# Output weight loaded behind the second exchange, and the last FP4 weight pieces loaded by GpSimd's queue

## The chip, the cores and the metric

One core of a Trainium2 chip runs the whole kernel in one launch. The metric is the device time in microseconds (us); lower is better. Before the change three runs gave a median of 1065.6 us (1063.15 to 1066.27).

## The reference

x has 4 batches of 1024 tokens with 256 features, all in float32. Cut to what matters (rmsnorm multiplies by a weight):

```
xn = layernorm(x)
# branch 1: linear attention (8 heads of 128, chunks of 128), then a SwiGLU MLP (1024)
h = rmsnorm(xn, attn_norm_w);  q, k, v = h@Wq, h@Wk, h@Wv      # per head
for each chunk:  o = tril(q k^T) v + q S;   S = S + k^T v
y = xn + rmsnorm(o, attn_out_norm_w) @ Wo
h = rmsnorm(y, mlp_norm_w)
s = y + (silu(h@Wgate) * (h@Wup)) @ Wdown
# branch 2: FP4 network; fq rounds groups of 16 to the FP4 grid, scaled by the group's maximum
a = silu(fq(xn) @ fq(w_gate)^T) * (fq(xn) @ fq(w_up)^T)        # 704 wide
out = x + s * silu(fq(a) @ fq(w_down)^T)
```

## The kernel before

Every float32 product is made of three products of rounded parts (high and low), each weight and activation being split once: ScalarE writes the high part, VectorE subtracts it for the low part. All products go through `split_product`, whose line is L263.

**Stages.** The first half of the run is attention; the second half, from about 605 us, is the MLP and the FP4 network together (`networks`). Attention goes through 4 batches, each with 16 head steps: step j is head j % 8 of the half batch (512 tokens, a "block") j // 8. In step j TensorE makes the scores of step j (L720), the keys, queries and values of step j+1 and later (L263), the state products (L750), the output from the masked scores (L765) and from the states (L771), and the output projection of step j-2 (L263). ScalarE copies results out of PSUM, squares outputs for the norm (L962) and rounds high parts. VectorE masks scores (L1518), sums states (L1542), normalizes outputs (L1563, L1558), and between these does the statistics of the next block (L1248 and on) and the FP4 rounding.

**The exchange.** The state products need the keys with tokens on the partitions. Instead of transposing on TensorE, each step sends keys and normalized outputs through DRAM: SP writes them in one transfer of 512 KB (L406, `moved<-work`), waits for it, and reads them back in four of 128 KB (L414, `r_gate<-moved`); VectorE then transposes blocks of 32x32 (L1389 for keys, L1506 for outputs). `exchange(value)` waits for the reads of the exchange before, for ScalarE's permuted keys (`k_perm_ready`) and for the normalized output (`o_norm_ready`).

**What sets the order.** Every engine's program is written out by hand and is executed in order; engines meet at semaphores only. All transfers but three small ones at the start are issued by SP, so they stand in one queue. SP's part of a step is `attention_transfers(b, j, first, final)`: the exchange first, then in some steps gate and up weights (h == 0), the store of x2 (`kept`), of the quantized x (`kept_xq`), of the normed h2 (`kept_h2`), and the loads and stores of FP4 weight pieces. Ahead of the loop stand the loads of x and of the q, k and v weights, exchange 1, the output weight `Wo` (1 MB, L496) and x of block 1 (L498).

**The output weight.** `raw_out` is its landing place. ScalarE rounds half of it in each of head steps 0 and 1 of the first batch (`weight_out_hi`, L1032) and VectorE takes the rest in steps 1 and 2 (`weight_out_lo`, L1320). TensorE needs the first half in step 2 and the second in step 6.

**FP4 weight pieces.** The three FP4 weights are cut in six pieces, which are rounded to the grid and turned during attention. Pieces 0 and 1 stay on chip. Pieces 2 to 5 are stored in DRAM (`kept_w4`) and are read back in the last batch: pieces 2 and 3 (352 KB each, `raw_gate4`) in step 12 at L454, after the exchange and the two stores of that step; pieces 4 and 5 (384 KB each, `raw_down4`) in step 14 at L468 and L470. ScalarE rounds the first two in step 14 and the others in step 15 (L1022), VectorE follows (L1492).

**GpSimd** (`block.gpsimd`) clears buffers at the start, waits for the q, k and v weights, clears two more, and has then no work until it multiplies and adds the finished rows of the networks.

Of the kernel before, what the change touches and what calls it, by code (L numbers as in the profile page):

```python
# [13 lines left out]
P = 128  # L14
# [44 lines left out]
def build(nc, x, attn_w, Wq, Wk, Wv, Wo, out_w, mlp_w, Wgate, Wup, Wdown, w_gate, w_up, w_down, out):  # L59
    batches, tokens, D = x.shape  # L60
    HD = Wq.shape[1]
    H = HD // P
    KD = D // P
# [7 lines left out]
    CH = BANK // P  # L71
    TB = CH * P
    HALVES = tokens // TB
    BLOCKS = batches * HALVES
# [22 lines left out]
    with ctx:  # L97
# [285 lines left out]
        with nc.Block() as block:  # L383
            @block.sync
            def _(sp):
# [31 lines left out]
                def attention_transfers(b, j, first, final):  # L417
# [3 lines left out]
                    if not (final and j >= STEPS - LAG):  # L421
                        exchange(t0 + j + 2, t0 + j if not first or j else None,
                                 t0 + j - 1 if not first or j >= LAG else None)
                    if h == 0:
                        sp.wait_ge(gu_ready, n + 1)
                        if n:
                            sp.wait_ge(xq_stored, 16 * n)
                        else:
                            sp.wait_ge(h_turned, KD)
                        for i, w in enumerate((Wgate, Wup)):  # L430
                            sp.dma_start(gu_piece[:, i, :], w[s * P:(s + 1) * P, b * PIECE:(b + 1) * PIECE])\
                              .then_inc(gu_loaded, 16)
# [17 lines left out]
                    if final and j == STEPS - CH:  # L450
                        sp.wait_ge(piece_stored, 16 * (PIECES - 2))
                        sp.wait_ge(o_done, b * STEPS + STEPS - CH)
                        for k in range(KD):
                            sp.dma_start(raw_gate4[:, k, :], kept_w4[2 + k]).then_inc(w4_loaded, 16)  # L454
# [10 lines left out]
                    if final and j == STEPS - LAG:  # L465
                        sp.wait_ge(piece_stored, 16 * (PIECES - 2))
                        sp.wait_ge(xq_ready, BLOCKS)
                        sp.dma_start(raw_down4[0], kept_w4[4]).then_inc(down4_loaded, 16)  # L468
                        sp.wait_ge(h2_turned, BLOCKS)
                        sp.dma_start(raw_down4[1], kept_w4[5]).then_inc(down4_loaded, 16)  # L470
# [25 lines left out]
                sp.dma_start(raw_out, Wo.rearrange("(h p) n -> p h n", p=P)).then_inc(w_loaded[W_OUT], 16)  # L496
# [77 lines left out]
            def _(pool):  # L574
# [12 lines left out]
                pool.memset(x2, 0.0).then_inc(x2_summed, 1)  # L587

# [322 lines left out]
            def _(act):  # L911
# [157 lines left out]
                def attention(b, j, first, final):  # L1069
# [25 lines left out]
                    if first and j < 2:  # L1095
                        weight_out_hi(j)
# [678 lines left out]
```

## Time and profile before

| what | us |
|---|---|
| median of three runs | 1065.6 |
| the profiled execution | 1068.49 |
| its span, first to last instruction | 1066.8 |
| busy in it: TensorE | 1053.6 |
| busy: VectorE | 905.1 |
| busy: ScalarE | 525.6 |
| busy: GpSimd | 47.2 |

The mean granted TensorE clock was 0.995 of full speed. Times inside a profile are counted from the start of its span; the busy time of TensorE includes time at the lower clock. "SPq" are instructions of SP that issue transfers.

### The profile page before, as it was taken

To read this page: it belongs to the slowest core of one execution; us is meant where nothing else is said; L and a number is where in the kernel's file an instruction comes from. 1 tells how busy PE (TensorE), PEld (TensorE's weight loads), DVE (VectorE), ACT (ScalarE), POOL (GpSimd) and SP (SyncE) were. 2 spreads that over 40 slices of the span, in tenths; PEclk is the share of its full clock that TensorE was granted. 3 is DMA by queue.
4 is the path that set the end of the run, shared out by engine and by line. 5 is a ranking of instruction groups with operands and counts; after the bars stand their busy time and mean duration, and the time that the engine had idled before them with its cause. 6 is when DMAs were issued, how large, how long until landed. Compare 5 with 4: busy or idle time off the path is not lost.

```text
span 1066.8 us, 18798 instructions
## 1 busy us (share of the span) xinstructions
PE 1053.6 (99%) x6790; PEld 965.0 (90%) x6790; DVE 905.1 (85%) x1860; ACT 525.6 (49%) x1482; POOL 47.2 (4%) x68
## 2 busy tenths in 40 slices
PE   9899999999999999999999999999999999999998
PEld 6799999989998999999998889999999999999997
DVE  6788898888887888888887798889888888889887
ACT  6664655755646646557555534443333333243332
POOL 1000000000000000000000000101001010101010
PEclk9999999999999999999999899999999999999999
DMA  7455355455464563654446523243433233423213
GB/s 250 129 153 175 118 170 170 128 162 168 134 189 131 166 185 107 186 167 153 160 129 204 150 65 100 80 149 93 125 93 115 88 120 92 125 86 91 87 57 112
DMA packets 166220, 143.08 MB, mean 134 GB/s; under 512 B 28784, under 2 KB 162928, under 8 KB 166128
## 3 DMA queue, kind: packets, MB, share of 16 engines
q1 hardware_dynamic: 165440, 141.88, 43.4%
q8 instruction: 54, 0.88, 0.4%
q14 instruction: 38, 0.31, 0.1%
q10 hardware_dynamic: 688, 0.00, 0.0%
HBM read 77.27 MB, written 64.57 MB: 133 GB/s over the span
## 4 chain that ended last, share of the span: by engine, by line
PE 94%; DMA 2%; DVE 1%; ACT 1%; issue 1%; SPq 0%; POOL 0%; DVEq 0%; ACTq 0%; POOLq 0%
PE ps L263 72%; PE ps L720 5%; PE ps L765 5%; PE ps L771 5%; PE ps L750 4%; DMA moved<-work 1%; DMA r_gate<-moved 1%; PE ps L854 1%; PE ps L648 1%; PE ps L608 1%; SPq L414 0%; DVE work L1362 0%; DVE work L1389 0%; ACT work L962 0%; DVE work L1506 0%
## 5 line engine op out<-in xcount | busy, mean ns | idle before, releaser
L263 PE MATMUL ps<-r_k,r_gate_up 128*128 128x512 f32 x768 | 185.2, 391 | 0.7 <-DVE r_k L1571 0.7
L263 PEld LDWEIGHTS ps<-r_k,r_gate_up 128*128 128x128 f32 x768 | 141.5, 188 | 28.1 <-issue 0.9
L263 PE MATMUL ps<-r_o,onT 128*128 128x256 f32 x768 | 107.5, 289 | 0.0
L263 PE MATMUL ps<-r_h,r_k 128*128 128x512 f32 (+1 forms) x393 | 105.1, 403 | 0.0
L263 PEld LDWEIGHTS ps<-r_q,r_v 128*128 128x128 f32 x768 | 99.7, 191 | 4.9 <-DVE r_v L1639 0.3
L263 PE MATMUL ps<-r_q,r_v 128*128 128x256 f32 x768 | 102.3, 283 | 0.0
L263 PE MATMUL ps<-r_h,r_q 128*128 128x512 f32 x384 | 98.2, 391 | 0.0
L263 PE MATMUL ps<-r_v,r_h 128*128 128x512 f32 x384 | 97.5, 390 | 0.0
L263 PEld LDWEIGHTS ps<-r_o,onT 128*128 128x128 f32 x768 | 96.5, 191 | 0.1
L962 ACT ACTIVATE work<-ps 128x128 f32<-128x128 f32 x256 | 67.1, 278 | 59.4 <-PE ps L771 59.3
L942 ACT ACTIVATE work<-ps 128x512 f32<-128x512 f32 x63 | 37.7, 598 | 111.3 <-PE ps L263 110.9
L1147 ACT ACTIVATE r_v<-work 128x512 fp32r<-128x512 f32 x64 | 40.5, 633 | 99.1 <-DVE work L1635 99.0
L263 PEld LDWEIGHTS ps<-r_h,r_q 128*128 128x128 f32 x384 | 72.1, 188 | 16.4
L263 PEld LDWEIGHTS ps<-r_v,r_h 128*128 128x128 f32 x384 | 72.1, 188 | 15.0
L1542 DVE TENSOR_TENSOR work<-ps,work 128x128 f32<-128x128 f32 x192 | 55.7, 290 | 32.0 <-ACT work L976 21.8
L263 PEld LDWEIGHTS ps<-r_h,r_k 128*128 128x128 f32 x393 | 68.3, 189 | 11.1
L1143 ACT ACTIVATE work<-ps 128x512 f32<-128x512 f32 x64 | 38.3, 598 | 79.7 <-PE ps L263 79.7
L263 PE MATMUL ps<-r_up,r_k 128*128 128x352 f32 x384 | 71.7, 322 | 0.2 <-DVE work L1558 0.2
L263 PE MATMUL ps<-r_gate,r_k 128*128 128x352 f32 x384 | 71.8, 322 | 0.0
L750 PEld LDWEIGHTS ps<-work 128*128 128x128 f32 x448 | 60.8, 195 | 12.1 <-DVE work L1389 3.9
L765 PE MATMUL ps<-work 128*128 128x128 f32 x512 | 69.3, 280 | 0.0
L750 PE MATMUL ps<-work 128*128 128x128 f32 x448 | 62.0, 280 | 5.8 <-DVE work L1389 3.1
(160 smaller groups left out, 2002.9 us busy)
## 6 DMA issues: line engine op xcount, KB each, us to landing
moved<-work SPq DMA_DIRECT2D x63, 512.0 KB, 2.9
r_gate<-moved SPq DMA_DIRECT2D x252, 128.0 KB, 2.6
kept_h<-work SPq DMA_DIRECT2D x31, 384.0 KB, 2.6
work<-kept_h SPq DMA_DIRECT2D x124, 96.0 KB, 2.3
work<-in_L_attn_hidden_states SPq DMA_DIRECT2D x15, 512.0 KB, 5.4
kept<-work SPq DMA_DIRECT2D x9, 514.0 KB, 4.9
kept_h<-work SPq DMA_DIRECT2D x9, 512.0 KB, 3.7
kept_xq<-work SPq DMA_DIRECT2D x8, 512.0 KB, 5.8
```

The source lines that it names most:

```text
L263: done = pe.matmul(out_ap, a, b, start=first and n == 0, stop=last and n == 2, skip_group_check=skip)
L608: done = pe.transpose(ps[:, H_BANKS[k], c * P:(c + 1) * P], h_sb[:, c, k * P:(k + 1) * P], ident[:, :])
L648: pe.matmul(ps[:, B_O, :], leaving[:, 0, 1, :], leaving[:, :, 1, :], start=True, stop=True)
L720: done = pe.matmul(ps[:, B_SCORE, c * P:(c + 1) * P], kT[:, c * P:(c + 1) * P], qT[:, j % 2, c * P:(c + 1) * P], start=True, stop=True)
L750: done = pe.matmul(ps[:, B_STATE, c * P:(c + 1) * P], k_tok[:, c, :], v_sb[:, half, c, hv:hv + P], start=True, stop=True)
L765: pe.matmul(ps[:, B_O, c * P:(c + 1) * P], attn[:, c, :], v_sb[:, half, c, hv:hv + P], start=c == 0, stop=s == 0 and c == 0, skip_group_ch ...
L771: done = pe.matmul(ps[:, B_O, c * P:(c + 1) * P], qT[:, j % 2, c * P:(c + 1) * P], before, start=False, stop=True, skip_group_check=True)
L942: act.activation(k_perm, ps[:, B_K, :].rearrange("p (c b t) -> p c b t", b=QUADS, t=QUAD), ACT.Copy)\
L962: done = act.activation(squares[:, c, :], ps[:, B_O, c * P:(c + 1) * P], ACT.Square, accum_out=small[:, OS, c:c + 1])
L1143: act.activation(s_gate, ps[:, B_GATE, :], ACT.Silu).then_inc(s_gate_ready, 1)
L1147: act.activation(hmT[:, f % 2, HI, :], hm, ACT.Copy).then_inc(hm_hi, 1)
L1542: dve.tensor_tensor(to, share, last, ALU.add).then_inc(state_ready, 1)
```

## The change

The load of `Wo` moves from behind exchange 1 to step 0 of the first batch, behind exchange 2 and ahead of that step's gate and up weights. ScalarE's two `weight_out_hi` move from steps 0 and 1 to steps 1 and 2. The four loads of `raw_gate4` and `raw_down4` leave SP's program; GpSimd issues them on its own queue, after the same waits, behind its second pair of clears.

```diff
--- before.py
+++ after.py
@@ -421,6 +421,8 @@
                     if not (final and j >= STEPS - LAG):
                         exchange(t0 + j + 2, t0 + j if not first or j else None,
                                  t0 + j - 1 if not first or j >= LAG else None)
+                    if (b, j) == (0, 0):
+                        sp.dma_start(raw_out, Wo.rearrange("(h p) n -> p h n", p=P)).then_inc(w_loaded[W_OUT], 16)
                     if h == 0:
                         sp.wait_ge(gu_ready, n + 1)
                         if n:
@@ -447,11 +449,6 @@
                         sp.wait_ge(xq_stored, 16)
                         sp.wait_ge(x2_summed, BLOCKS)
                         load_turned(xq_in, kept_xq[0], xq_loaded)
-                    if final and j == STEPS - CH:
-                        sp.wait_ge(piece_stored, 16 * (PIECES - 2))
-                        sp.wait_ge(o_done, b * STEPS + STEPS - CH)
-                        for k in range(KD):
-                            sp.dma_start(raw_gate4[:, k, :], kept_w4[2 + k]).then_inc(w4_loaded, 16)
                     if h == CH + 1:
                         sp.wait_ge(h2_turned, n + 1)
                         sp.dma_start(kept_h2[(n + BLOCKS - 1) % BLOCKS].rearrange("a p x -> p a x"), in_quads(h_flat))\
@@ -462,12 +459,6 @@
                         else:
                             sp.wait_ge(w_ready, W_OUT + 2)
                         load_piece(n, range(QUADS // 2) if h == CH + 1 else range(QUADS // 2, QUADS))
-                    if final and j == STEPS - LAG:
-                        sp.wait_ge(piece_stored, 16 * (PIECES - 2))
-                        sp.wait_ge(xq_ready, BLOCKS)
-                        sp.dma_start(raw_down4[0], kept_w4[4]).then_inc(down4_loaded, 16)
-                        sp.wait_ge(h2_turned, BLOCKS)
-                        sp.dma_start(raw_down4[1], kept_w4[5]).then_inc(down4_loaded, 16)
 
                 def load_piece(m, quads):
 
@@ -493,7 +484,6 @@
                         sp.dma_start(in_quads(to)[q * QUAD:(q + 1) * QUAD],
                                      quads[q].rearrange("(b p) x -> p b x", b=QUADS)).then_inc(done_sem, 16)
                 exchange(1, again=False)
-                sp.dma_start(raw_out, Wo.rearrange("(h p) n -> p h n", p=P)).then_inc(w_loaded[W_OUT], 16)
                 sp.wait_ge(xn_ready, 1)
                 sp.dma_start(x_in, x_blocks[1]).then_inc(x_loaded, 16)
                 for j in range(ROLL):
@@ -585,6 +575,16 @@
                 pool.wait_ge(w_ready, W_OUT)
                 pool.memset(attn, 0.0).then_inc(attn_cleared, 1)
                 pool.memset(x2, 0.0).then_inc(x2_summed, 1)
+
+                last = (batches - 1) * STEPS
+                pool.wait_ge(piece_stored, 16 * (PIECES - 2))
+                pool.wait_ge(o_done, last + STEPS - CH)
+                for k in range(KD):
+                    pool.dma_start(raw_gate4[:, k, :], kept_w4[2 + k]).then_inc(w4_loaded, 16)
+                pool.wait_ge(xq_ready, BLOCKS)
+                pool.dma_start(raw_down4[0], kept_w4[4]).then_inc(down4_loaded, 16)
+                pool.wait_ge(h2_turned, BLOCKS)
+                pool.dma_start(raw_down4[1], kept_w4[5]).then_inc(down4_loaded, 16)
 
                 pool.sem_inc(product_ready, 1)
                 for n in range(BLOCKS - 1):
@@ -1092,8 +1092,8 @@
                         copy_v(t0 + j + CH + 1, *((1, h) if h < CH else (0, h - CH)))
                     if s == 0:
                         first_state(t0 + j + 1, b * UPDATES + updates_before(j))
-                    if first and j < 2:
-                        weight_out_hi(j)
+                    if first and j in (1, 2):
+                        weight_out_hi(j - 1)
                     if h == 1:
                         wgate_up_hi(b, s)
                     if h == 2:
```

## Rows read from the trace of the kernel before

**Rows 1.** The page, busy share (part 1) and chain (part 4).

```profile
PE 1053.6 (99%) x6790; PEld 965.0 (90%) x6790; DVE 905.1 (85%) x1860; ACT 525.6 (49%) x1482; POOL 47.2 (4%) x68
...
PE 94%; DMA 2%; DVE 1%; ACT 1%; issue 1%; SPq 0%; POOL 0%; DVEq 0%; ACTq 0%; POOLq 0%
```

**Rows 2.** Timeline of TensorE: start us, us, engine line op out<-in xcount [idle before <-releaser].

```profile
29.94 1.52 PE L263 MATMUL ps<-r_v,r_h 128*128 128x512 f32 x6
34.56 1.88 PE L750 MATMUL ps<-work 128*128 128x128 f32 x8 [3.10 <-DVE work L1389]
36.23 1.92 PE L765 MATMUL ps<-work 128*128 128x128 f32 x8
...
43.74 1.05 PE L750 MATMUL ps<-work 128*128 128x128 f32 x8
44.63 1.06 PE L765 MATMUL ps<-work 128*128 128x128 f32 x8
...
53.12 1.05 PE L750 MATMUL ps<-work 128*128 128x128 f32 x8
...
328.77 1.21 PE L771 MATMUL ps<-work 128*128 128x128 f32 x6 [0.34 <-ACT work L976]
```

**Rows 3.** Slices of half a us: busy (x) of each engine, granted clock, DMA share, GB/s.

```profile
34.50:35.00 0.50, 0.44 (x3) 0.44 (x4) 0.00 (x1) 0.00 (x0) 0.00 (x0) 0.80 0.68 238
```

**Rows 4.** Timeline of SP's queue, first exchanges.

```profile
19.08 0.43 SPq L496 DMA_DIRECT2D work<-in_L_attn_Wo  x1
...
22.00 0.37 SPq L406 DMA_DIRECT2D moved<-work  x1
28.82 1.75 SPq L414 DMA_DIRECT2D r_gate<-moved  x4
```

**Rows 5.** The page, part 6: issue, KB each, median us to landing.

```profile
moved<-work SPq DMA_DIRECT2D x63, 512.0 KB, 2.9
```

**Rows 6.** Timeline of VectorE, first head steps.

```profile
27.48 1.41 DVE L1248 BATCH_NORM_STATS2 work<-work 128x6 f32<-128x256 f32 x4 [1.26 <-DMA work<-in_L_attn_hidden_states]
...
32.52 0.16 DVE L1272 TENSOR_TENSOR work<-work 128x4 f32<-128x4 f32 x1
33.79 0.71 DVE L1389 STREAM_TRANSPOSE work<-r_gate 128x512 f32<-128x512 f32 x1 [1.11 <-DMA r_gate<-moved]
...
52.15 0.71 DVE L1389 STREAM_TRANSPOSE work<-r_gate 128x512 f32<-128x512 f32 x1
```

**Rows 7.** Timeline of ScalarE, head steps 1 and 2.

```profile
36.65 1.14 ACT L1032 ACTIVATE r_o<-work,nw_out 128x1024 fp32r<-128x1024 f32 x1
...
47.39 0.26 ACT L962 ACTIVATE work<-ps 128x128 f32<-128x128 f32 x1
```

**Rows 8.** Timeline of SP's queue, head step 12 of the last batch.

```profile
575.24 2.25 SPq L454 DMA_DIRECT2D work<-kept_w  x2
577.60 0.56 SPq L406 DMA_DIRECT2D moved<-work  x1
583.74 1.74 SPq L414 DMA_DIRECT2D r_gate<-moved  x4
```

**Rows 9.** Timelines of TensorE and of VectorE at the second stop.

```profile
588.41 1.62 PE L750 MATMUL ps<-work 128*128 128x128 f32 x6 [2.72 <-issue]
...
587.60 0.71 DVE L1389 STREAM_TRANSPOSE work<-r_gate 128x512 f32<-128x512 f32 x1 [2.50 <-DMA r_gate<-moved]
```

**Rows 10.** Slices of half a us at attention's end.

```profile
576.50:577.00 0.50, 0.50 (x4) 0.41 (x3) 0.50 (x2) 0.24 (x1) 0.00 (x0) 1.00 0.97 366
...
587.50:588.00 0.50, 0.00 (x0) 0.00 (x0) 0.40 (x1) 0.00 (x0) 0.00 (x0) 0.76 1.06 328
...
594.50:595.00 0.50, 0.50 (x6) 0.50 (x5) 0.01 (x1) 0.47 (x4) 0.00 (x0) 0.92 0.00 0
```

**Rows 11.** Timeline of ScalarE, rounding of the last pieces.

```profile
589.95 1.46 ACT L1022 ACTIVATE r_gate<-work 128x704 fp32r<-128x704 f32 x2
...
597.32 1.58 ACT L1022 ACTIVATE r_h<-work 128x768 fp32r<-128x768 f32 x2
```

## The prediction

> **What bounds the kernel now.** I read the page's busy shares and its chain first: TensorE is busy 99% of the span, and the chain that ended last is 94% TensorE [rows 1]. Time can come only from places where TensorE stands still or runs slowly. Its timeline up to 600 us has two stops longer than 0.4 us behind the start-up: 3.10 us ahead of the state products at 34.56 [rows 2] and 2.72 us at 588.41 [rows 9]. Each edit works on one of them.
>
> Both stops cost more than their length. After the first the granted clock is 0.80 in the slice 34.5 to 35.0 [rows 3] and 0.50 in those that follow: 1.2 instead of 2.4 GHz. The same eight products take 1.88 us at 34.56 and 1.05 at 43.74, the next eight 1.92 and 1.06 [rows 2]: 0.83 + 0.86 = 1.7 us lost, of which about 0.1 hides a wait on the states. At the second stop the clock falls in the slice 587.5 to 588.0 and is back in the slice 594.5 to 595.0 [rows 10]. By the slice means that is about 587.76 to 594.54; the work from 588.41 on is 6.1 us at half rate, so 3.1 us are lost.
>
> I call the exchange that brings head step j its exchange j+1. The loop's step j issues exchange j+2.
>
> **Why the first stop exists.** SP issues the output weight (1 MB) at 19.08, x behind it, and exchange 2's write at 22.00 [rows 4]. That write's issue waits for ScalarE's permuted key, not for the weight. Its reads start at 28.82 [rows 4], so it took 6.8 us; the median of 63 such writes is 2.9 [rows 5]. VectorE transposes at 33.79 [rows 6], TensorE goes on at 34.56.
>
> **Part 1, the weight behind exchange 2.** Without 1 MB ahead, the write takes 2.9 us, or up to 3.8 with the tail of x ahead, and the reads are issued from 25.0 to 25.8. From first read issue to transpose the row has 33.79 - 28.82 = 5.0 us, so the tile is there between 30.0 and 30.8 [rows 4, 6]. Then VectorE is late. Its statistics of the next block began at 27.48 after 1.26 us of waiting for x [rows 6], which also stood behind the weight. With x there they begin at 26.2. From their start to the end of the last small operation ahead of the transpose are 32.52 + 0.16 - 27.48 = 5.2 us, in which nothing waits [rows 6]. So the transpose starts at 31.4, and TensorE, which followed it by 34.56 - 33.79 = 0.77, at 32.1 to 32.2. Gain 2.4 us. TensorE's values end at 29.94 + 1.52 = 31.46 [rows 2], so a stop of 0.7 us is left. A stop of 0.34 us at 328.77 [rows 2] left the clock at 1.0, one of 3.1 did not; I take it that 0.7 does, and the 1.6 us come back as well. Bounds of the clock term: 0 and 1.7.
>
> The rounding of the weight (ScalarE, 1.14 us a half [rows 7]; VectorE 1.2) moves from head steps 0 and 1 to 1 and 2. In step 0 this frees ScalarE, which nobody waits for there. In step 1 the first half takes the place of the second: no change in length, VectorE's part follows right behind. In step 2 there is 1.05 us (1.14 less the overlap of neighbours) of new work ahead of the squares of x2 and of the root of the output norm, which began at 47.39 [rows 7]. VectorE had been late for that root by about 0.1, as it normalized the next block until 49.0, so 0.9 us pass on to its chain and its transpose of step 3. That transpose ran 52.15 to 52.86 [rows 6], 0.26 ahead of TensorE's need at 53.12 [rows 2]; the first state copy and state sums of that step, which the state products need at once, shift by the full 0.9. I take a loss of 0.9 us for TensorE; bounds 0 (if the slack takes it) and 1.2.
>
> The weight is now ahead of exchange 3, with 256 KB of gate and up weights. It is issued at 26.8 to 27.6; 1.25 MB at the 366 GB/s of [rows 10] take 3.6 us and end at 31.4 to 32.3. Exchange 3's write is issued at 29.8 (behind the norm of step 0), lands at 33.3 to 34.1, and its reads (5.0 us) are there by 38.3 to 39.1. VectorE gets to that transpose at 38.5 in the moved time line, TensorE needs its end at 39.8. So the cover is 0.1 to 0.7 us: I take a cost of 0. If it is gone, it costs one for one, up to 2.0 if the weight runs at the pace it had at 19.08, where it shared the engines.
>
> Sum of part 1: -2.4 - 1.6 + 0.9 = -3.1 us.
>
> **Part 2, the FP4 pieces on GpSimd's queue.** In head step 12 of the last batch SP issues two loads of 352 KB at 575.24, then the write of exchange 15 at 577.60, whose reads start only at 583.74 [rows 8]: 6.1 us instead of 2.9. VectorE's transpose follows at 587.60 and TensorE at 588.41 [rows 9]. VectorE itself would be ready at about 585.0, so this stop ends with the transfer throughout. The change takes 0.72 MB out from ahead of that write: they start some 10 us sooner, when step 11's output is done (about 564.9). It puts the first 384 KB of the down weight there instead: GpSimd issues it when the quantized x is turned, about 573.7. The second 384 KB go at about 581.4, between the write's data and its reads. At 366 GB/s [rows 10] that is 2.0 us out and 1.1 in: the write lands 0.9 us sooner, and the stop is 1.8 us. I take -0.9. The bounds: nothing gained or 1 us lost where GpSimd's loads run beside the reads of exchanges 13 and 14, whose transposes have under 0.4 us of cover; and -2.0 if the down piece slips in beside. For the clock I take no change: it fell 2.1 us after the products had stopped, and 1.8 is near.
>
> What comes late now is no risk: ScalarE rounds the pieces at 589.95 and 597.32 [rows 11], 25 and 16 us behind their issue. GpSimd has nothing else to do until the gated products of the networks, so its three new waits block nobody.
>
> The trace of before has no load on GpSimd's queue. The Trainium skill (DMA: Bandwidth & Descriptors, Queues, rings and completion order) says that each DMA engine takes turns between its queues packet by packet. By that rule the bulk loads, which on SP's queue stood in line, take half the engines from an exchange issued beside them; those are cases 3 and 5 below. The skill also says (SBUF - State Buffer, SBUF: two separate sides) that GpSimd cannot write descriptors while VectorE runs certain fast copies. With 16 us of cover and more that changes no number here.
>
> **The sum.** -3.1 - 0.9 = -4.0 us against the profiled execution: 1068.5 (span 1066.8, and 1.7 around it) gives 1064.5. The median of the runs shown is 2.9 us under that execution, so I put it at 1065.6 - 4.0 = 1061.6 us. What a measurement of this kernel can tell from no change is about 0.3%, or 3.2 us.
>
> **The cases.** Four rivals stand around the forecast.
> 1. Both stops shrink and the second leaves the clock up: 3.1 us more. 1061.6 - 3.1 = 1058.5. For it: the stop falls under the 2.1 us after which the clock fell. Against: it is only 0.3 us under, and a stop of 0.7 us would be a safer sign than one of 1.8. 0.20.
> 2. The forecast as above, 1061.6; with its own bounds 1060 to 1063.2. 0.37.
> 3. GpSimd's loads give nothing: they take from exchanges 13 and 14 what they free for 15, and cost 0.4 on top. 1065.6 - 3.1 + 0.4 = 1062.9. For it: these transposes have almost no cover. 0.20.
> 4. The weight wait only moves to exchange 3: 2.0 us of a new stop at step 2. 1061.6 + 2.0 = 1063.6. For it: only 0.1 to 0.7 us of cover. Against: the weight meets an emptier queue than at 19.08. 0.13.
> 5. Slower. GpSimd's bulk gets its share of the engines at the cost of the exchanges one for one: 0.72 MB ahead of exchange 14's write is 2.0 us, two pieces of 0.39 MB are 1.1 each, 4.2 together less 0.4 of cover; the 0.9 is not gained, and a second fall of the clock adds 3.1. 1065.6 - 3.1 + 3.8 + 3.1 = 1069.4. It decides once the exchanges lose more than about 3 us. Against: between 567.5 and 570 the engines are half idle, which takes most of the gate piece. 0.10.
>
> **How the numbers follow.** Faster by over 0.3% (under 1062.4): all of case 1, 0.26 of case 2, 0.03 of case 3: 0.49. Slower: case 5, 0.10. The rest, 0.41, is within. The range 1058.0 to 1064.8 leaves out case 5 and the far side of case 1.
>
> **What would show it.** In the trace of after: exchange 2's write lands in about 3 us; TensorE's first stop is 0.7 us, ends right behind a VectorE transpose that did not wait for a transfer, and the clock stays at 1.0; the values of step 1 start about 4 us earlier than before; at the state products of step 3 0.9 us of that are gone. At the end of attention the stop is 1.8 us and still ends with exchange 15's reads. I am wrong if exchange 3's transpose waits for its transfer, if there are new stops in steps 12 and 13, or if the shift between the traces at 500 us is not near 3 us.

## The result: slower by 0.27%, where 0.4% faster was forecast

The changed kernel's median is 1068.38 us, the kernel before's on the same chip 1065.93 us (14 runs each): a ratio of 1.0027 with a 95% interval of 1.0015 to 1.0038. A second study gave 1.0014 (1.0002 to 1.0026). Ratios here and below stand as they were recorded; they differ from the quotient of the two medians by up to 0.001. The forecast was 1061.6 us, with a range that ended at 1064.8.

The profiled execution took 1071.52 us, the longest of the 14, with a span of 1069.6. The busy shares are those of before. In the page's chain transfers hold 6% instead of 2% [rows 1], and TensorE 87% instead of 94%.

```profile
PE 87%; DMA 6%; DVE 2%; SPq 2%; ACT 1%; issue 1%; ACTq 0%; DVEq 0%
...
moved<-work SPq DMA_DIRECT2D x63, 512.0 KB, 2.9
```

Both lines are traps. The shares do not tell before from after: the second profile of the changed kernel has TensorE at 90%, part 2 alone, which is slower than before, has 94%, and the three profiles under 90% are those with the longest middle stretch (below), where no edit works. And the median of the 63 writes is 2.9 us as in [rows 5]. Single ones have to be read.

**The first stop.** TensorE's timeline of after (columns as in [rows 2]):

```profile
32.06 1.16 PE L750 MATMUL ps<-work 128*128 128x128 f32 x8 [0.70 <-DVE work L1389]
33.06 1.06 PE L765 MATMUL ps<-work 128*128 128x128 f32 x8
...
42.35 1.36 PE L750 MATMUL ps<-work 128*128 128x128 f32 x8 [2.54 <-DVE work L1389]
43.50 1.92 PE L765 MATMUL ps<-work 128*128 128x128 f32 x8
...
52.98 1.11 PE L750 MATMUL ps<-work 128*128 128x128 f32 x8
```

The stop of 3.10 us is 0.70 now, and the products behind it run at full rate (1.16 and 1.06 us where [rows 2] have 1.88 and 1.92). At 42.35 TensorE is still 1.39 us ahead of the time line of before, although it has just stood for 2.54 us. That stop is new, and behind it the eight products of L765 take 1.92 us. At step 3 (52.98 against 53.12) almost all of the gain is gone. VectorE and ScalarE show where the new stop comes from:

```profile
31.30 0.71 DVE L1389 STREAM_TRANSPOSE work<-r_gate 128x512 f32<-128x512 f32 x1
...
41.58 0.71 DVE L1389 STREAM_TRANSPOSE work<-r_gate 128x512 f32<-128x512 f32 x1 [1.04 <-DMA r_gate<-moved]
```

```profile
35.26 1.15 ACT L1032 ACTIVATE r_o<-work,nw_out 128x1024 fp32r<-128x1024 f32 x1 [1.73 <-DMA work<-in_L_attn_Wo]
```

The transpose of step 1 waited for no transfer, as forecast. The next one did, and ScalarE had stood still for the weight before that. SP's queue has the lengths:

```profile
21.91 0.38 SPq L406 DMA_DIRECT2D moved<-work  x1
26.25 1.75 SPq L414 DMA_DIRECT2D r_gate<-moved  x4
28.03 0.43 SPq L425 DMA_DIRECT2D work<-in_L_attn_Wo  x1
...
30.33 0.38 SPq L406 DMA_DIRECT2D moved<-work  x1
37.62 1.75 SPq L414 DMA_DIRECT2D r_gate<-moved  x4
```

Exchange 2's write took 26.25 - 21.91 = 4.3 us instead of 6.8. Exchange 3's, with the weight ahead of it, took 37.62 - 30.33 = 7.3. The weight itself, as the list of transfers of after has it (last number: us from issue to landing); in the trace of before it took 5.8:

```profile
work<-in_L_attn_Wo SPq DMA_DIRECT2D x1, 1024.0 KB, 7.2
```

**The end of attention.** SP's queue and GpSimd's:

```profile
567.68 2.92 SPq L484 DMA_DIRECT2D work<-kept_xq  x4
571.76 0.38 SPq L406 DMA_DIRECT2D moved<-work  x1
577.32 1.76 SPq L414 DMA_DIRECT2D r_gate<-moved  x4
...
582.47 0.36 SPq L406 DMA_DIRECT2D moved<-work  x1
586.35 1.74 SPq L414 DMA_DIRECT2D r_gate<-moved  x4
```

```profile
567.89 1.25 POOL L583 DMA_DIRECT2D work<-kept_w  x2 [547.08 <-PE ps L771]
576.42 0.54 POOL L585 DMA_DIRECT2D work<-kept_w  x1 [7.29 <-DVE work L1362]
587.52 0.54 POOL L587 DMA_DIRECT2D work<-kept_w  x1 [10.56 <-DVE work L1362]
```

The gate pieces are issued 3.9 us ahead of exchange 14's write, which takes 5.6 us; in the trace of before it took 3.0:

```profile
569.47 0.38 SPq L406 DMA_DIRECT2D moved<-work  x1
572.46 1.73 SPq L414 DMA_DIRECT2D r_gate<-moved  x4
```

The write of exchange 15 takes 3.9 instead of 6.1 [rows 8]. So the stop ahead of step 14 [rows 9] is gone and one of the same size stands a step earlier. The next three fences are TensorE, VectorE and two slices (columns as in [rows 3]):

```profile
583.28 1.62 PE L750 MATMUL ps<-work 128*128 128x128 f32 x6 [2.74 <-issue]
```

```profile
582.47 0.71 DVE L1389 STREAM_TRANSPOSE work<-r_gate 128x512 f32<-128x512 f32 x1 [3.33 <-DMA r_gate<-moved]
```

```profile
572.00:572.50 0.50, 0.50 (x5) 0.34 (x4) 0.50 (x2) 0.19 (x1) 0.00 (x0) 1.00 0.82 295
...
583.00:583.50 0.50, 0.22 (x1) 0.25 (x2) 0.50 (x2) 0.00 (x0) 0.00 (x0) 0.50 1.06 371
```

**Three stretches.** To compare all traces I cut each into three parts by TensorE's timeline: the start (to the state products of step 4), the middle (from there to those of step 12 of the last batch) and attention's end (from there to the first product of the networks, L263 with `r_k,r_gate_up`). What follows took 458.3 to 458.5 us in every trace.

| kernel | start | middle | end |
|---|---|---|---|
| before | 62.91 | 507.02 | 38.52 |
| after | 62.85 | 509.37 | 39.06 |
| after, second profile | 60.88 | 507.70 | 39.12 |

The middle is touched by no edit. In the first profile of after it is 2.35 us longer than before, in the second 0.68. All fourteen traces of this study lie between 505.6 and 509.8 there, without order by edit. So one pair of profiles can't account for the difference of two medians; below the edited stretches are compared over all traces. At the end both profiles of after are 0.5 to 0.6 us longer than this one trace of before.

### The profile page after: what moved, and what is told of

The parts are those of the page before. It is cut to its first block, busy times and chain, and to the rows that moved or that the text cites. A ratio compares the mean times of both kernels' runs of the same rounds, so it can differ in the third digit from the quotient of the medians.

```text
span 1069.6 us, 18797 instructions
## 1 busy us (share of the span) xinstructions
PE 1054.8 (99%) x6790; PEld 964.8 (90%) x6790; DVE 906.0 (85%) x1860; ACT 525.1 (49%) x1482; POOL 49.7 (5%) x72
## 4 chain that ended last, share of the span: by engine, by line
PE 87%; DMA 6%; DVE 2%; SPq 2%; ACT 1%; issue 1%; ACTq 0%; DVEq 0%
PE ps L263 68%; PE ps L720 5%; PE ps L771 4%; PE ps L765 4%; DMA moved<-work 4%; PE ps L750 4%; DMA r_gate<-moved 2%; SPq L414 1%; PE ps L854 1%; PE ps L608 1%; SPq L480 1%; DVE work L1389 0%; DVE work L1506 0%; DMA work<-in_L_attn_hidden_states 0%; ACT work L942 0%
## 5 line engine op out<-in xcount | busy, mean ns | idle before, releaser
L263 PE MATMUL ps<-r_k,r_gate_up 128*128 128x512 f32 x768 | 185.2, 391 | 0.7 <-DVE r_k L1571 0.7
L263 PEld LDWEIGHTS ps<-r_k,r_gate_up 128*128 128x128 f32 x768 | 141.6, 188 | 28.1 <-issue 0.9
L263 PE MATMUL ps<-r_o,onT 128*128 128x256 f32 x768 | 107.5, 290 | 0.0
L263 PE MATMUL ps<-r_h,r_k 128*128 128x512 f32 (+1 forms) x393 | 105.2, 403 | 0.0
L263 PEld LDWEIGHTS ps<-r_q,r_v 128*128 128x128 f32 x768 | 99.7, 191 | 4.9 <-DVE r_v L1639 0.3
L263 PE MATMUL ps<-r_q,r_v 128*128 128x256 f32 x768 | 102.3, 283 | 0.0
L263 PE MATMUL ps<-r_h,r_q 128*128 128x512 f32 x384 | 98.2, 391 | 0.0
L263 PE MATMUL ps<-r_v,r_h 128*128 128x512 f32 x384 | 97.4, 391 | 0.0
L263 PEld LDWEIGHTS ps<-r_o,onT 128*128 128x128 f32 x768 | 96.6, 191 | 0.1
L263 PEld LDWEIGHTS ps<-r_h,r_q 128*128 128x128 f32 x384 | 72.2, 188 | 16.4
L263 PEld LDWEIGHTS ps<-r_v,r_h 128*128 128x128 f32 x384 | 72.1, 188 | 14.9
L1542 DVE TENSOR_TENSOR work<-ps,work 128x128 f32<-128x128 f32 x192 | 55.8, 291 | 31.2 <-ACT work L976 21.3
L263 PEld LDWEIGHTS ps<-r_h,r_k 128*128 128x128 f32 x393 | 68.3, 189 | 11.0
L263 PE MATMUL ps<-r_up,r_k 128*128 128x352 f32 x384 | 71.7, 322 | 0.2 <-DVE work L1558 0.2
L263 PE MATMUL ps<-r_gate,r_k 128*128 128x352 f32 x384 | 71.8, 323 | 0.0
L765 PE MATMUL ps<-work 128*128 128x128 f32 x512 | 69.4, 280 | 0.0
L771 PE MATMUL ps<-work 128*128 128x128 f32 x448 | 67.4, 289 | 1.2 <-DVE work L1542 0.6
```

The costliest lines, as they stand in the source:

```text
L263: done = pe.matmul(out_ap, a, b, start=first and n == 0, stop=last and n == 2, skip_group_check=skip)
L765: pe.matmul(ps[:, B_O, c * P:(c + 1) * P], attn[:, c, :], v_sb[:, half, c, hv:hv + P], start=c == 0, stop=s == 0 and c == 0, skip_group_ch ...
L771: done = pe.matmul(ps[:, B_O, c * P:(c + 1) * P], qT[:, j % 2, c * P:(c + 1) * P], before, start=False, stop=True, skip_group_check=True)
L1542: dve.tensor_tensor(to, share, last, ALU.add).then_inc(state_ready, 1)
```

## The experiments

Every kernel below was timed together with the kernel before on the same chip. "Part 1" is the change of `Wo` and of ScalarE's two `weight_out_hi`, "part 2" the move of the four loads to GpSimd, both as in the diff of the change.

**Each part alone.** Part 1 without part 2, on one chip and once more on another:

```diff
-                sp.dma_start(raw_out, Wo...)           # behind exchange 1
+                    if (b, j) == (0, 0):               # behind exchange 2
+                        sp.dma_start(raw_out, Wo...)
-                    if first and j < 2:
-                        weight_out_hi(j)
+                    if first and j in (1, 2):
+                        weight_out_hi(j - 1)
```

> Part 1 alone: the output weight behind exchange 2, the FP4 pieces as before. Theory A (the wait only moves: 1.25 MB stand ahead of exchange 3's write): exchange 3's write takes about 7 us, TensorE stands 0.7 us in step 1 and about 2.5 us in step 2, the clock falls behind the second of these, and from step 3 on the state products start within 0.3 us of before; time within 1 us of before (ratio 0.999 to 1.001). Rival B (most of the 2.4 us that the changed kernel lost in steps 25 to 42, which no edit touches, come from part 1 through another alignment of transfers): 2 us or more slower than before, and the same steps show the shift again.

> Part 1 alone, again, on the chip of the changed kernel. If the parts add up: part 1 alone is 0.5 to 2 us faster than before and the changed kernel equals the sum of this and part 2 alone within 1.5 us. If they don't: part 1 alone is faster as in its first run and the changed kernel is 2 us or more over the sum.

Measured: 1064.43 us against 1065.75, ratio 0.9987 (0.9977 to 0.9998), and on the other chip 1065.78 against 1066.24, ratio 0.9998 (0.9987 to 1.0009). Part 1 gains between nothing and 1.4 us, where 3.1 were forecast. The mechanism of theory A was there, at under half the size that it named: the stop was 1.11 us, not 2.5, and the clock stayed up. The two timelines agree on why. SP's queue of the first:

```profile
27.39 0.43 SPq L425 DMA_DIRECT2D work<-in_L_attn_Wo  x1
...
30.00 0.38 SPq L406 DMA_DIRECT2D moved<-work  x1
35.97 1.75 SPq L414 DMA_DIRECT2D r_gate<-moved  x4
```

Exchange 3's write takes 6.0 us here and 6.4 in the repetition, and leaves stops ahead of step 2 of 1.11 and 0.81 us:

```profile
40.65 1.16 PE L751 MATMUL ps<-work 128*128 128x128 f32 x8 [1.11 <-DVE work L1390]
...
51.26 1.16 PE L751 MATMUL ps<-work 128*128 128x128 f32 x8 [0.55 <-DVE work L1390]
```

Part 2 without part 1, on the same two chips:

```diff
-                    if final and j == STEPS - CH:      # SP: both gate pieces (L454)
-                    if final and j == STEPS - LAG:     # SP: both down pieces
...
+                pool.wait_ge(o_done, last + STEPS - CH)
+                for k in range(KD):
+                    pool.dma_start(raw_gate4[:, k, :], kept_w4[2 + k]).then_inc(w4_loaded, 16)
+                pool.wait_ge(xq_ready, BLOCKS)
+                pool.dma_start(raw_down4[0], kept_w4[4]).then_inc(down4_loaded, 16)
+                pool.wait_ge(h2_turned, BLOCKS)
+                pool.dma_start(raw_down4[1], kept_w4[5]).then_inc(down4_loaded, 16)
```

> Part 2 alone: all four FP4 pieces on GpSimd's queue, the output weight as before. Theory A (the gate pieces, issued about 10 us sooner, meet exchange 14 as they met exchange 15 before): exchange 14's write takes about 5.5 us instead of 3, the stop of 2.7 us stands ahead of step 13 and not of step 14, and step 15 starts 0.3 to 0.8 us later than before: 0.5 us slower, ratio 1.000 to 1.001. Rival B (all of the 2.5 us of the change come from here): ratio 1.002 or more. Rival C (my forecast of this part): 0.9 us faster with the stop ahead of step 14.

> Part 2 alone, again, on the chip of the changed kernel. As in its first run: 1 to 2.5 us over before, the stop of about 3 us ahead of step 13, and 38.8 us from step 60 to the networks. If it comes out within 0.5 us of before, the loss of the changed kernel needs both parts together.

Measured: 1068.05 against 1065.75, ratio 1.0017 (1.0005 to 1.0030); on the other chip 1068.07 against 1066.24, ratio 1.0016 (1.0002 to 1.0029). Part 2 is the slower half, and by the ratios it costs 1.8 and 1.7 us. Exchange 14's write took 5.9 and 5.4 us, and TensorE stood ahead of step 13 for 2.96 and 3.11 us. Theory A had the place and the length of this stop, but a price of 0.5 us. The end took 37.91 us the second time, not 38.8. TensorE's timeline of the first:

```profile
580.24 1.07 PE L749 MATMUL ps<-work 128*128 128x128 f32 x6 [2.96 <-issue]
590.19 0.91 PE L749 MATMUL ps<-work 128*128 128x128 f32 x6 [0.56 <-issue]
```

**The changed kernel once more**, beside the repetitions of its parts:

> The changed kernel again, beside each of its parts on one chip. Theory A (the 2.4 us that its first profile lost in steps 4 to 60, where no edit works, are one execution's): this profile takes 505.6 to 507.0 us from step 4 to step 60 like most others; the two ends repeat, 37.8 to 39.2 us from step 0 to 4 and 38.8 to 39.1 from step 60 to the networks; time 0 to 1.5 us over before. Rival B (the change itself slows the middle, by where the exchanges fall against the other transfers): 509 us or more again, and 2.5 us or more over before.

Measured: 1067.3 against 1066.24, ratio 1.0014 (1.0002 to 1.0026). The product of its parts on that chip is 0.9998 x 1.0016 = 1.0014: on it they add up. On the chip of their first runs the product is 1.0004, while the first study of the change measured 1.0027 (1.0015 to 1.0038); so the sum is shown on one chip only. Two of the three expected stretches missed: 36.9 us from step 0 to step 4, and 507.7 in the middle; the end with 39.1 did not. Exchange 3's write took 35.45 - 29.88 = 5.6 us this time, with a stop of 0.26 us instead of 2.54. So the price of the weight ahead of exchange 3 differs from execution to execution.

**The weight in halves.** If the 1 MB ahead of exchange 3 is what costs, half of it ahead of exchange 3 and half behind must give the forecast gain. Against part 1 (each half has a semaphore of its own, for which ScalarE waits; cut here):

```diff
-                    if (b, j) == (0, 0):
-                        sp.dma_start(raw_out, Wo...)
+                    if (b, j) in ((0, 0), (0, 1)):
+                        half = slice(j * CH, (j + 1) * CH)
+                        sp.dma_start(raw_out[:, half, :], Wo...[:, half, :]).then_inc(w_loaded[W_OUT + j], 16)
```

> Part 1 with the output weight in two loads of 512 KB, one behind exchange 2 and one behind exchange 3 (each with a semaphore of its own). Theory A (exchange 3 is late by the bytes ahead of it): 0.5 MB less at about 300 GB/s, so its write lands 1.7 us sooner, ScalarE's rounding in step 1 does not wait for the weight (1.7 us in the changed kernel), TensorE's stop ahead of step 2 is 0.3 to 1 us and the clock stays up; step 3 starts 2.5 to 3.5 us earlier than before; time 2 to 3.5 us under before. Rival B (the stop ahead of step 2 has another cause, for one the chain of the norm on ScalarE and VectorE): the stop stays over 2 us and the time equals before's.

Measured: 1063.78 against 1065.75, ratio 0.9983 (0.9972 to 0.9994): 1.8 us gained, just under the 2 to 3.5 of theory A. SP's queue and TensorE:

```profile
27.01 0.43 SPq L426 DMA_DIRECT2D work<-in_L_attn_Wo  x1
...
29.95 0.38 SPq L406 DMA_DIRECT2D moved<-work  x1
33.87 1.75 SPq L414 DMA_DIRECT2D r_gate<-moved  x4
35.66 0.43 SPq L426 DMA_DIRECT2D work<-in_L_attn_Wo  x1
```

```profile
39.96 1.05 PE L753 MATMUL ps<-work 128*128 128x128 f32 x8
...
50.31 1.16 PE L753 MATMUL ps<-work 128*128 128x128 f32 x8 [0.55 <-DVE work L1392]
```

Exchange 3's write is down to 3.9 us and TensorE does not stop for it. Step 4 comes 2.63 us earlier than in the trace of before, 0.5 short of the forecast's 3.1.

**The gate pieces behind exchange 15.** Part 2 wanted this transfer out of exchange 15's way. The plainest way leaves everything on SP and swaps the order:

```diff
-                    if final and j == STEPS - CH:
+                    if final and j == STEPS - CH + 1:
```

> The kernel before with one edit: the two gate pieces (352 KB each) are issued by SP behind exchange 15 instead of ahead of its write. Theory A (that write is late by the bytes ahead of it): it lands about 2 us sooner, the stop ahead of step 14 is 0.7 us instead of 2.7; if the clock then stays up, 3 us more come back: 4 to 5 us faster; if it still falls, 2 us. Rival B (the stores of x2 and of the quantized x alone hold the write up, or the pieces then land too late for ScalarE in step 14): under 1 us faster or slower than before, with ScalarE waiting for the pieces in step 14.

Measured: 1062.54 against 1065.75, ratio 0.9971 (0.9957 to 0.9984). SP's queue and TensorE:

```profile
575.02 0.36 SPq L406 DMA_DIRECT2D moved<-work  x1
578.00 1.74 SPq L414 DMA_DIRECT2D r_gate<-moved  x4
579.84 0.85 SPq L454 DMA_DIRECT2D work<-kept_w  x2
```

```profile
575.48 0.83 PE L750 MATMUL ps<-work 128*128 128x128 f32 x6
...
583.26 0.91 PE L750 MATMUL ps<-work 128*128 128x128 f32 x6
```

The write takes 3.0 us, and no stop is left ahead of steps 13 to 15. The gain is 3.1 us, under the 4 to 5 of theory A.

**Which piece, and which queue.** Three kernels take part 2 apart. Only the gate pieces on GpSimd:

```diff
-                    if final and j == STEPS - CH:      # SP: both gate pieces
+                pool.wait_ge(o_done, last + STEPS - CH)
+                for k in range(KD):
+                    pool.dma_start(raw_gate4[:, k, :], kept_w4[2 + k]).then_inc(w4_loaded, 16)
```

> Only the two gate pieces on GpSimd's queue, at the output of step 11; the down pieces stay with SP in step 14, the output weight as before. Theory A (the gate pieces make the loss of part 2): exchange 14's write takes 5.5 to 6 us, a stop of 2.5 to 3 us ahead of step 13 as with all four pieces, no stop ahead of step 14; time 0.5 to 1.8 us over before. Rival B (the down pieces on that queue make it): exchange 14's write 3 to 4 us, no stop ahead of step 13, and, as 0.7 MB are gone from ahead of exchange 15, 3 us faster as with the pieces behind exchange 15.

Measured: 1065.73 against 1065.6, ratio 0.9994 (0.9981 to 1.0007). Exchange 14's write took 571.93 - 566.61 = 5.3 us, the stop ahead of step 13 is 1.87 us with the clock up, and none is left ahead of step 14. Theory A has the write and the place of the stop, but its loss of 0.5 to 1.8 us is not measured: the interval reaches from 2.0 us faster to 0.7 slower. The 3 us of rival B are not there either.

The same loads at about the same place, but by SP, ahead of exchange 14's write:

```diff
+                    if final and j == STEPS - CH:      # SP: both gate pieces, now ahead of exchange(...)
                     if not (final and j >= STEPS - LAG):
                         exchange(...)
-                    if final and j == STEPS - CH:      # SP: both gate pieces, at L454
```

> The two gate pieces issued by SP ahead of exchange 14's write, which is about when GpSimd issues them; the rest as before. Theory A (it is the time and the bytes, not the queue): exchange 14's write takes 5.5 us or more and the stop of 2.5 to 3 us stands ahead of step 13; time equals that of the gate pieces on GpSimd's queue within 1 us. Rival B (the queue itself does it: its own descriptors, or turns taken against SP's queue): the write takes 4 us or less and the stop is under 1.5 us, 2 us or more faster than with GpSimd's queue.

Measured: 1065.58 against 1065.6, ratio 1.0010 (0.9998 to 1.0021). Its queue:

```profile
570.74 0.85 SPq L425 DMA_DIRECT2D work<-kept_w  x2
571.70 0.37 SPq L406 DMA_DIRECT2D moved<-work  x1
577.78 1.74 SPq L414 DMA_DIRECT2D r_gate<-moved  x4
```

The stop ahead of step 13 is 2.26 us. The medians of the two kernels are 0.15 us apart, their ratios 0.0016 with overlapping intervals. The write takes 6.1 us behind the loads in one queue, 5.3 to 6.0 us beside them from another: 0.7 MB delay it from either queue. The two differ in the moment as well, though: SP issues the loads 1.0 us ahead of the write, behind the reads of `kept_xq`, GpSimd 3.9 us ahead, beside these reads. So no run shows what the queue alone does. The Trainium skill (DMA: Bandwidth & Descriptors, Queues, rings and completion order) says that each DMA engine serves its queues in turn, packet by packet. The traces agree as far as the second queue's load did not leave the write alone; the write is 0.1 to 0.8 us shorter beside it, and no more.

Only the down pieces on GpSimd, the gate pieces back at L454 on SP:

```diff
-                    if final and j == STEPS - LAG:     # SP: both down pieces
+                pool.wait_ge(xq_ready, BLOCKS)
+                pool.dma_start(raw_down4[0], kept_w4[4]).then_inc(down4_loaded, 16)
+                pool.wait_ge(h2_turned, BLOCKS)
+                pool.dma_start(raw_down4[1], kept_w4[5]).then_inc(down4_loaded, 16)
```

> Only the two down pieces on GpSimd's queue, the first when the quantized x is turned (step 12), the second when the normed h2 is turned (step 13); the gate pieces stay with SP ahead of exchange 15's write. Theory A (bytes issued ahead of an exchange's write delay it): 0.39 MB more stand ahead of exchange 15's write, which takes about 7 us instead of 6.1; the stop ahead of step 14 grows from 2.7 to 3.5 us, 0.8 to 1.1 us slower than before. Rival B (the down pieces are hidden): stop and time as before, within 0.4 us.

Measured: 1067.52 against 1065.6, ratio 1.0022 (1.0010 to 1.0034). GpSimd issues the first piece at 573.90, SP the gate pieces at 574.58, and all of it stands ahead of the same write. SP's queue and TensorE:

```profile
574.58 2.26 SPq L454 DMA_DIRECT2D work<-kept_w  x2
577.12 0.37 SPq L406 DMA_DIRECT2D moved<-work  x1
584.48 1.84 SPq L414 DMA_DIRECT2D r_gate<-moved  x4
```

```profile
589.79 1.62 PE L750 MATMUL ps<-work 128*128 128x128 f32 x6 [4.41 <-issue]
```

The write takes 7.4 us where 6.1 were taken with the gate pieces alone [rows 8], and the stop is 4.41 us instead of 2.72. At 2.3 us by the ratio the loss is twice what theory A gave it.

**GpSimd's queue, but late.** All four loads stay with GpSimd and wait until exchange 15's write has landed:

```diff
-                pool.wait_ge(o_done, last + STEPS - CH)
+                pool.wait_ge(moved_out, 16 * (last + STEPS - 1))
```

> All four FP4 pieces on GpSimd's queue, as in the change, but its first wait is for exchange 15's write to have landed, so that no piece stands ahead of or beside an exchange's write; the output weight as before. Theory A (the moment and the bytes cost, not the queue): no stop over 1 us ahead of steps 13 and 14, 3 us faster than before, as with the gate pieces behind exchange 15 on SP. Rival B (GpSimd's queue costs by itself, by its own descriptors or by turns against exchange 15's reads): a stop of over 1 us ahead of step 14, or under 1.5 us faster than before.

Measured: 1065.91 against 1066.24, ratio 1.0001 (0.9985 to 1.0017): better than part 2, 3 us short of the same order on SP. The write is back at 3.0 us (579.63 to 582.61). Then the two queues run together. GpSimd's first loads (the down pieces follow at 584.36 and 584.88) and VectorE's transpose:

```profile
583.12 1.25 POOL L582 DMA_DIRECT2D work<-kept_w  x2 [562.91 <-DMA moved<-work]
```

```profile
589.09 0.71 DVE L1388 STREAM_TRANSPOSE work<-r_gate 128x512 f32<-128x512 f32 x1 [2.59 <-DMA r_gate<-moved]
```

From the first read's issue to the transpose are 589.09 - 582.61 = 6.5 us, where [rows 8, 9] have 3.9, and TensorE stands for 2.00 us ahead of step 14. With the same pieces on SP's queue, issued 1.8 us behind the first read and not 0.5 as here, it was 4.5 us, and there was no stop. Whether the queue or the moment makes this difference was not separated: a load of GpSimd's that waits until all the reads are issued was not run.

**The better version.** The weight in halves and the gate pieces behind exchange 15, both edits as shown above:

> The output weight in two halves (behind exchanges 2 and 3) and the gate pieces behind exchange 15 on SP, both in one kernel. Theory A (two independent waits for transfers, each shortened by what stands ahead of an exchange's write): the gains add, 1.8 + 3.1 = 5 us under before, ratio 0.995 to 0.996; no stop over 1 us in steps 1 to 3 nor ahead of step 14. Rival B (the clock or later steps give one of them back): ratio 0.997 or more.

Measured: 1060.85 us against 1065.6, ratio 0.9955 (0.9943 to 0.9967), which beats both kernels; 0.9983 x 0.9971 = 0.9954 is what its two edits gave alone. Its write of exchange 3 is followed by no stop, and its write of exchange 15 takes 3.2 us.

**The stretches over all traces.** With all fourteen profiles the start and the end can be read as groups (us, one execution each):

| stretch and kernels | each | mean |
|---|---|---|
| start, weight as before | 62.91 63.03 63.07 62.51 62.38 60.88 60.68 60.28 | 61.97 |
| start, part 1 | 62.85 61.21 61.56 60.88 | 61.63 |
| start, weight in halves | 60.28 60.65 | 60.47 |
| end, pieces as before | 38.52 37.53 37.20 35.70 | 37.24 |
| end, part 2 | 39.06 38.82 39.12 37.91 | 38.73 |
| end, gate pieces behind exchange 15 | 33.71 33.35 | 33.53 |
| end, gate pieces alone on GpSimd | 35.55 | |
| end, gate pieces by SP ahead of exchange 14 | 37.19 | |
| end, down pieces alone on GpSimd | 39.00 | |
| end, all four on GpSimd, late | 35.75 | |

By these means part 1 gives 0.3 us, the halves give 1.5, part 2 costs 1.5, and the late gate pieces give 3.7; the timed ratios say 0.2 to 1.4, 1.8, 1.7 to 1.8 and 3.1.

The first row holds something that the single trace of before could not show. With the same start of the program, the stop ahead of step 1 was 3.10 us in the trace of the forecast and 3.27, 2.94, 3.87, 3.30, 2.39, 1.82 and 2.15 us in the others. The granted clock fell in four of the eight: while TensorE stood (2.94), as it went on (3.10 and 3.27) and 1.4 us after that (3.87). It stayed up in the other four. The way from the state products of step 1 to those of step 2 has the price: 7.57 to 7.60 us with the clock up, 9.18 to 9.21 in three of the four and 10.35 in the fourth (2.94). TensorE's timeline of the kernel with only the gate pieces moved to behind exchange 15:

```profile
33.71 1.16 PE L750 MATMUL ps<-work 128*128 128x128 f32 x8 [1.82 <-DVE work L1389]
```

## Why the prediction was wrong, step by step

**Part 1's steps up to exchange 2: right.** The stop was to shrink to 0.7 us and did (0.70, and 0.67 to 0.69 in the other traces with that order). The transpose was forecast at 31.4 without a wait for the transfer and ran at 31.30. The write took 4.3 us where up to 3.8 were allowed, which cost nothing, since VectorE was the later. The clock stayed up.

**"I take a cost of 0" for exchange 3: this failed.** I had the write landing at 33.3 to 34.1, by letting 1.25 MB run at 366 GB/s, the rate of one busy slice [rows 10]. (By my own numbers they would have ended at 30.4 to 31.2, not 31.4 to 32.3.) The 1 MB of the weight alone landed 7.2 us behind its issue, where I gave 3.6 to all 1.25 MB. The write landed at 37.6, and at 35.5 to 36.4 in three more executions: 5.6 to 7.3 us instead of 3.5 to 4.3. I had seen this price in [rows 4], 6.8 us with the same megabyte ahead, and put it down to what the weight shared the engines with at that moment, instead of to the megabyte. With 512 KB less ahead the write took 3.9 us, which is the experiment that shows the cause. My bound of "up to 2.0" was about right: the stops were 2.54, 1.11, 0.81 and 0.26 us, 1.2 in the mean. Behind the one of 2.54 the clock fell, and the sixteen products there took 1.36 + 1.92 us instead of 1.05 + 1.06. That cost the step nothing: the state products of step 3 followed those of step 2 by 10.63 us, and by 10.59 to 10.61 where the clock stayed up and TensorE waited for ScalarE instead.

**ScalarE's +0.9: right in size.** Where exchange 3 did not hide it, new stops of 0.34 and 0.55 us stand in step 2 and ahead of step 3. The halves have 0.20 and 0.55. From step 2 to step 3 this is 10.6 us instead of 9.6 with the clock up: 1.0 us.

**The clock term of -1.6 was read from one execution.** Its size was right where the clock fell, but it fell in four of eight traces with the same start, so in the mean before had 0.9 us of it. The profiled execution of before was 2.9 us above its kernel's median, and both stops had the clock fall in it. I carried this 2.9 over as a constant. Against the means of the table its start was 0.9 us and its end 1.3 us long, so most of it was part of what the change was to remove. That fits with the halves, which are 2.6 us earlier against that trace and gain 1.8 us in the median. With the means of all traces the sum of part 1 (first stop, clock, ScalarE, exchange 3) is -2.2 - 0.9 + 1.0 + 1.2 = -0.9 us, between the two timed gains; without the 1.2 of exchange 3 it is -2.1.

**Part 2's -0.9: this failed too, with its sign.** The freeing of exchange 15 went further than forecast (write 3.9 us, no stop instead of 1.8). But I put exchange 14's share at nothing, since the engines were half idle between 567.5 and 570. The loads were issued at 567.89 together with SP's reads of `kept_xq` (567.68). They landed 5.9 us behind their issue, the reads 5.8 where they took 3.4 in before, and the engines were still at 0.82 of their time in the slice from 572.0, behind the write's issue at 571.76. It took 5.6 us. "New stops in steps 12 and 13" was the sign I had named for being wrong; one came in step 13, 2.74 us long, with the clock down from 582.5 to 589.3. Case 5 had this mechanism for 1069.4 us at a chance of 0.10, and case 4 the other half. That both could come together was in none of the cases, and this is what happened: 0.2 to 1.4 us gained by part 1, 1.8 lost by part 2.

**The down pieces: not only what they do to a write.** With the gate pieces alone on GpSimd the ratio is 0.9994, with all four 1.0016 and 1.0017; between them lie about 2 us. In the four traces with all four pieces the first down piece is issued 0.9 to 1.4 us ahead of exchange 14's reads, and from the first of these reads to VectorE's transpose, which waits for them, are 4.8 to 5.4 us. With the gate pieces alone on GpSimd it is 4.1:

```profile
576.07 0.71 DVE L1390 STREAM_TRANSPOSE work<-r_gate 128x512 f32<-128x512 f32 x1 [2.45 <-DMA r_gate<-moved]
```

The second down piece goes out 1.2 to 1.3 us behind exchange 15's first read. Three of the four traces have 5.9 to 6.5 us from there to a transpose that waits, against 4.0, and two of them stops of 0.56 and 0.99 us ahead of step 14. The prediction had this only as a bound ("nothing gained or 1 us lost where GpSimd's loads run beside the reads of exchanges 13 and 14"). The rest may be the clock, which fell behind the stop ahead of step 13 in all four and not behind the one of 1.87 us; that is one profile, and not shown.

What stays open is why the first study has the change 1.4 to 2.4 us above the sum of its parts (noise is not excluded), and what makes the middle longer in some executions. In the first profile of after all of its 2.35 us come between steps 31 and 42, and TensorE shows no stop above 0.34 us there. One trace of it is on record: the three executions with the longest middle (509.4 to 509.8) are the only ones in which the exchange's write behind SP's loads of `w_down`, issued at 380 to 382 us there, took 4.8 to 5.2 us. In the eleven others it took 3.5 to 3.6. That would be the wait of the edits once more, a write behind bulk loads; that it makes the middle longer, and what sets it off, is not shown.

## What to carry to other kernels

When a bulk load delays a short transfer that the critical engine needs, moving it one exchange earlier or later, or to another queue, only chose the next victim here (between the queues, no run kept the moment the same). What worked was to put it directly behind the reads of the last exchange that could spare it, on the same queue, and in two pieces where one delayed the next exchange's write. Price a transfer behind a megabyte by the row that shows one behind a megabyte, not by bytes over peak rate. And where a profile lies 3 us above the median and the effect is 4 us, ask which of its stops the median execution has at all.

## What was not expected of the hardware

- After stops of similar length the clock fell in some executions and not in others. It stayed up behind 1.82, 1.87, 2.00, 2.15, 2.38, 2.39 and 3.30 us; it fell behind 2.26, 2.47, 2.54, 2.68, 2.72, 2.74, 2.83, 2.94, 2.96, 3.10, 3.11, 3.27, 3.87 and 4.41. Between 2.26 and 3.30 us these traces hold both, so the price of such a stop belongs in a forecast with a chance.
- The time of a 512 KB write goes with what was issued in the 4 us ahead of it. Exchange 15's, with the gate pieces elsewhere, took 3.0 us where 1 MB of stores had been issued 3.1 to 3.6 us ahead, 3.2 at 2.6 to 3.1 us, and 4.0 at 1.7 to 2.4 us. Exchange 3's took 3.9 and 4.0 with 0.75 MB of loads issued 1.9 to 2.9 us ahead (the halves). With 1.2 to 2.1 MB, among them the whole output weight or the gate pieces, writes took 5.3 to 7.8 us.
- One load issued on GpSimd's queue kept that engine 0.54 us for a 384 KB load (0.71 once) and 0.62 for a 352 KB one, close to SP's 0.43. SP needed 0.85 us for the same two loads behind exchange 15's reads, and 2.25 us where they stand in the kernel before [rows 8]; what held it up there was not looked into.
